# GpSimd waits for its gathers at every second group of tiles in the six edge passes of a graph network kernel

## The chip, the cores and the metric

The kernel runs on one core of one Trainium2 chip. The metric is the device time of a whole execution in microseconds (us). Three runs of the kernel before gave 10969.36, 11014.58 and 11011.19 us; the median is 11011.19 us.

## The reference, cut to what matters

A graph of N = 6250 nodes with 128 float32 features and E = 100000 edges passes through four layers, each fed by a layer norm and a ReLU and added to the running features.

```python
# layer 0: messages by edge type, gated by a sigmoid, summed over the target node, then a GRU cell
msg_in = concat([x[src], x[dst]], axis=1)
h = relu(msg_in @ W1[t] + b1[t]);  m = (h @ W2[t] + b2[t]) * sigmoid(msg_in @ attn_w[t] + attn_b[t])
agg = zeros_like(x).at[dst].add(msgs)
# layer 1: attention over the edges of a row (sorted by src), softmax per row
score = neighs @ high - 0.5 * (neighs @ diff)      # neighs = tanh(x)[dst]; here rows = src
out = segment_sum(neighs * softmax_per_row(score)[:, None], rows)
# layer 2: relations with 8 bases
msg = sum_b w_comp[etype, b] * (x[src] @ weight[b]) * norm;  out = relu(segment_sum(msg, dst) + bias + x @ loop)
# layer 3: three graph convolutions with symmetric degree norm, one after the other
out = segment_sum((x @ W)[src] * norm[:, None], dst) + b
```

Every layer gathers a row of a table for each edge and sums the results per node. Nothing in the change touches what is computed.

## The kernel before, in words

All of it is float32. The kernel first sorts the edges by target window (128 nodes) with counting and scatters them into "slots": 832 tiles of 128 edges, in which each tile belongs to one window; the tiles that are left over at the end are padding, whose slots hold index 0 and a key that matches nothing. A second sort by source serves layer 1. Between the sorts and the passes lie stages that build tables in HBM.

There are six passes over the edges, each a scope of its own with its own semaphores: `edges0`, `edges1`, `edges2`, and `edges3` once for each of three graph convolutions. A pass goes through GROUPS = 208 groups of G = 4 tiles. In each pass GpSimd does nothing but the gathers, through the helper `gather_groups`: for each tile an indirect DMA (line 484) brings 128 rows of a table in HBM into a ring of buffers in SBUF, one row for each of the 128 partitions.

- `edges0` gathers two tables (`rows_s` and `rows_d`, rows of 132 floats, 528 bytes), so eight gathers a group; the ring has R = 4 groups. VectorE adds the two (line 791), ScalarE makes the hidden values (774, 777), VectorE makes one-hot matrices of the target and type (799), TensorE multiplies (851) and VectorE adds the product into the accumulator (815). A slot of the ring is free again when `hidden_done` counts its group.
- `edges1` gathers one table with rows of 528 bytes; the ring has eight groups. ScalarE takes the landed rows first (1133); VectorE, TensorE and ScalarE work out a running softmax. A slot is free with `sums`.
- `edges2` gathers rows of 1024 floats, 4096 bytes (eight bases); the ring has four groups. When a group has landed, ScalarE scales four of the eight parts (1424) and VectorE the others (1447, 1459), VectorE makes the one-hot (1436), TensorE multiplies six parts for each tile (1492), and VectorE adds (1469). A slot is free with `product`.
- `edges3` gathers rows of 128 floats, 512 bytes; the ring has eight groups. TensorE multiplies the one-hot (1602) by the landed rows (1623) and VectorE adds (1612). A slot is free with `product`.

Each slot of the ring has its own semaphore `gathered[slot]`; a gather adds 16 to it when it has landed. The consumers wait until it has reached 16 x (gathers of a group) x (turns of the ring). The order of GpSimd's work is that of its program: for each group the wait for a free slot, then its gathers. The other engines run through the stages of a group as software pipelines with fixed lags, written by `for_groups`.

Of the kernel before, what the change touches and what calls it, by code (L numbers as in the profile page):

```python
# [43 lines left out]
G, R, R1 = 4, 4, 8  # L44
# [387 lines left out]
def wait(engine, semaphore, value):  # L432

    if not isinstance(value, int) or value > 0:
        engine.wait_ge(semaphore, value)
# [39 lines left out]
def gather_groups(pool, ring, freed, gathered, parts):  # L475


    for g in range(GROUPS):
        slot = g % ring
        wait(pool, freed, g - ring + 1)  # L480
        for j in range(G):
            for rows, table, slots, field in parts:
                index = slots[:, G * g + j, field:field + 1].bitcast(I32)
                pool.indirect_dma_start(out=rows[:, slot, j, :], out_offset=None, in_=table[:, :],  # L484
                                        in_offset=bass.IndirectOffsetOnAxis(ap=index, axis=0)).then_inc(gathered[slot], 16)
# [236 lines left out]
def edges0(nc, A, D, K, acc):  # L722


    with Scope(nc, "edge0") as s:
# [31 lines left out]
        @block.gpsimd  # L757
        def _(pool):
            gather_groups(pool, R, q["hidden_done"], gathered,
                          [(rows_s, D["tab_src"], slots, F_SRCT), (rows_d, D["tab_dst"], slots, F_DSTT)])  # L760
# [319 lines left out]
def edges1(nc, D, K, acc):  # L1080
# [5 lines left out]
    with Scope(nc, "edge1") as s:  # L1086
# [28 lines left out]
        @block.gpsimd  # L1115
        def _(pool):
            pool.wait_ge(q["indexed"], 1)
            gather_groups(pool, R1, q["sums"], gathered, [(rows, D["tab1"], slots, 0)])
# [270 lines left out]
def edges2(nc, D, K, acc):  # L1389
# [7 lines left out]
    with Scope(nc, "edge2") as s:  # L1397
# [13 lines left out]
        @block.gpsimd  # L1411
        def _(pool):
            gather_groups(pool, R, q["product"], gathered, [(rows, D["tab2"], slots, F_SRC)])
# [326 lines left out]
```

## Time and profile before

| | |
|---|---|
| median of three runs | 11011.19 us |
| profiled execution | 10982.13 us |
| its span, first to last instruction | 10980.3 us |
| mean granted TensorE clock | 0.708 of full |
| busy: PE, DVE, ACT, POOL | 52%, 48%, 22%, 69% |
| HBM traffic | 80 GB/s over the span |

The engines are named as in the profile: PE is TensorE's matmul and PEld its weight load, DVE VectorE, ACT ScalarE, POOL GpSimd. Busy time leaves out waits. In the span edges0 lies at about 1630 to 3960 us, edges1 at 5045 to 6120, edges2 at 6342 to 7515, and the three layers of edges3 begin at 7607, 8740 and 9880.

### The profile page before, as it was taken

To read this page: it belongs to the slowest core of one execution; us is meant where nothing else is said; L and a number is where in the kernel's file an instruction comes from. 1 tells how busy PE (TensorE), PEld (TensorE's weight loads), DVE (VectorE), ACT (ScalarE), POOL (GpSimd) and SP (SyncE) were. 2 spreads that over 40 slices of the span, in tenths; PEclk is the share of its full clock that TensorE was granted. 3 is DMA by queue.
4 is the path that set the end of the run, shared out by engine and by line. 5 is a ranking of instruction groups with operands and counts; after the bars stand their busy time and mean duration, and the time that the engine had idled before them with its cause. 6 is when DMAs were issued, how large, how long until landed. Compare 5 with 4: busy or idle time off the path is not lost. (4 is left out here: it accounts for less than half of the span.)

```text
span 10980.3 us, 128933 instructions
## 1 busy us (share of the span) xinstructions
PE 5704.4 (52%) x31462; PEld 4939.8 (45%) x31462; DVE 5292.9 (48%) x11473; ACT 2403.8 (22%) x7643; POOL 7613.1 (69%) x7650
## 2 busy tenths in 40 slices
PE   0000646667666667603566689995444344434443
PEld 0000326666666655402555389995333333333332
DVE  6931016555555531134666578886333433343333
ACT  1000101111111111104767378883000000000000
POOL 1276767777777777777777267774777577757775
PEclk9999657888888865556767799997555555555555
DMA  9901122222222210002222399994222322221223
GB/s 21 16 6 24 62 65 50 50 50 50 50 50 50 50 23 2 2 14 49 53 53 53 92 356 382 381 385 145 52 52 52 47 52 52 52 49 52 52 52 53
DMA packets 587441, 879.48 MB, mean 80 GB/s; under 512 B 340739, under 2 KB 377041, under 8 KB 586828
## 3 DMA queue, kind: packets, MB, share of 16 engines
q0 software_dynamic: 329728, 772.96, 24.5%
q1 hardware_dynamic: 257612, 105.52, 10.1%
q14 instruction: 80, 0.66, 0.0%
q8 instruction: 21, 0.34, 0.0%
HBM read 791.80 MB, written 86.16 MB: 80 GB/s over the span
## 5 line engine op out<-in xcount | busy, mean ns | idle before, releaser
L484 POOL DMA_INDIRECT edge_rows<-tab,all_slots x3328 | 3212.8, 965 | 1113.2 <-issue 976.1
L1623 PE MATMUL edge_psum<-edge_rows,edge_onehot 128*128 128x128 f32 x4992 | 1290.8, 440 | 1908.9 <-DMA edge_rows<-tab,all_slots 1694.1
L1623 PEld LDWEIGHTS edge_psum<-edge_rows,edge_onehot 128*128 128x128 f32 x4992 | 1111.1, 328 | 2088.3 <-issue 1874.0
L1612 DVE TENSOR_TENSOR acc_acc<-acc_acc,edge_psum 128x128 f32 x2496 | 716.4, 287 | 2041.4 <-PE edge_psum L1623 1770.9
L851 PE MATMUL edge_psum<-edge_hidden,edge_onehot 128*128 128x130 f32 x6656 | 1176.4, 354 | 800.1 <-ACT edge_hidden L777 794.2
L851 PEld LDWEIGHTS edge_psum<-edge_hidden,edge_onehot 128*128 128x128 f32 x6656 | 1120.9, 264 | 866.1 <-DVE acc_acc L815 754.2
L1492 PE MATMUL edge_p_m<-edge_rows,edge_onehot 128*128 128x128 f32 x9984 | 1130.5, 276 | 46.9 <-ACT edge_rows L1424 42.6
L1492 PEld LDWEIGHTS edge_p_m<-edge_rows,edge_onehot 128*128 128x128 f32 x9984 | 1122.2, 192 | 55.3 <-issue 33.8
L484 POOL DMA_INDIRECT edge_rows_d<-tab_dst,all_slots x832 | 958.0, 1151 | 253.7 <-issue 253.7
L484 POOL DMA_INDIRECT edge_rows_s<-tab_src,all_slots x832 | 852.5, 1025 | 275.3 <-issue 253.4
L1424 ACT ACTIVATE edge_rows<-edge_rows,edge_coef 128x128 f32<-128x128 f32 x3328 | 997.6, 390 | 173.5 <-DMA edge_rows<-tab,all_slots 173.5
L484 POOL DMA_INDIRECT edge_rows<-tab,edge_slots x832 | 811.0, 975 | 262.3 <-issue 253.4
L196 POOL DMA_INDIRECT slots_s<-upd_pay_ring,upd_row_ring x656 | 632.6, 964 | 229.8 <-issue 206.4
L815 DVE TENSOR_TENSOR acc_acc<-acc_acc,edge_psum 128x520 f32 x832 | 576.5, 693 | 310.4 <-PE edge_psum L851 261.4
L1567 ACT ACTIVATE tab_hT<-tab_p_t 128x128 f32<-128x128 f32 x150 | 41.5, 278 | 2273.0 <-PE tab_p_t L1553 2271.3
L1266 PE MATMUL edge_p_u<-edge_rows,edge_prob 128*128 128x129 f32 x1664 | 355.0, 379 | 318.7 <-ACT edge_prob L1159 318.7
L196 POOL DMA_INDIRECT slots_d<-sort_pay_ring,sort_row_ring x320 | 358.3, 1120 | 218.3 <-DMA sort_pay_ring<-pay_d 120.5
L799 DVE TENSOR_TENSOR edge_onehot<-all_iota,all_slots 128x1024 f32<-128x1024 f32 x416 | 507.8, 1221 | 0.0
L1459 DVE SCALAR_TENSOR_TENSOR edge_rows<-edge_rows,edge_coef 128x128 f32<-128x128 f32 x1664 | 487.5, 344 | 0.0
L196 POOL DMA_INDIRECT slots_d<-tab_pay_ring,tab_row_ring x400 | 384.2, 961 | 145.7 <-issue 122.9
L774 ACT ACTIVATE edge_hidden<-edge_rows_s 128x4 f32<-128x4 f32 x208 | 43.9, 211 | 1984.4 <-DVE edge_rows_s L791 1984.4
L1266 PEld LDWEIGHTS edge_p_u<-edge_rows,edge_prob 128*128 128x128 f32 x1664 | 301.2, 271 | 382.9 <-ACT edge_prob L1159 338.5
(250 smaller groups left out, 8590.1 us busy)
## 6 DMA issues: line engine op xcount, KB each, us to landing
edge_rows<-tab,all_slots POOLq DMA_INDIRECT x3328, 2.5
tab<-tab_o SPq DMA_DIRECT2D x50, 512.0 KB, 2.6
edge_rows_s<-tab_src,all_slots POOLq DMA_INDIRECT x832
edge_rows_d<-tab_dst,all_slots POOLq DMA_INDIRECT x832
edge_rows<-tab,edge_slots POOLq DMA_INDIRECT x832, 2.5
tab_src<-tab_oa SPq DMA_DIRECT2D x50, 264.0 KB, 2.1
tab_dst<-tab_ob SPq DMA_DIRECT2D x50, 264.0 KB, 2.2
slots_s<-upd_pay_ring,upd_row_ring POOLq DMA_INDIRECT x656
```

Of the source, the lines that this page charges most:

```text
L196: pool.indirect_dma_start(out=self.table[:, :], out_offset=bass.IndirectOffsetOnAxis(ap=self.row_ring[:, z, j:j + 1], axis=0), in_=self.pa ...
L484: pool.indirect_dma_start(out=rows[:, slot, j, :], out_offset=None, in_=table[:, :], in_offset=bass.IndirectOffsetOnAxis(ap=index, axis=0) ...
L774: act.activation(hidden[:, slot % 2, :, H], rows_s[:, slot, :, H], ACT.Sigmoid).then_inc(q["scored"], 1)
L799: v.tensor_tensor(onehot[:, slot % 2, half * n:(half + 1) * n, :], bcast_mid(K["iota"][:, :], n), bcast_last(slots[:, ds(g * G + half * n, ...
L815: v.tensor_tensor(at, at, psum[:, j % 2, :, 0:2 * SW], ALU.add).then_inc(q["added"], 1)
L851: m = pe.matmul(psum[:, j % 2, t // 2, (t % 2) * SW:(t % 2) * SW + SW], onehot[:, slot % 2, j, t * P:(t + 1) * P], hidden[:, slot % 2, j, ...
L1266: m = pe.matmul(p_u[:, z, j // 2, (j % 2) * HW:(j % 2) * HW + H + 1], prob[:, z, j, :], rows[:, slot, j, 0:H + 1], start=True, stop=True)
L1424: a = act.activation(part, part, ACT.Copy, scale=coef[:, ds(G * g + j, 1), b])
L1459: v.scalar_tensor_tensor(first, rows[:, slot, j, b * H:(b + 1) * H], coef[:, ds(G * g + j, 1), b], first, ALU.mult, ALU.add).then_inc(q["c ...
L1492: m = pe.matmul(at, onehot[:, z, j, :], rows[:, slot, j, b * H:(b + 1) * H], start=(n == 0), stop=(n == len(PARTS) - 1))
L1612: v.tensor_tensor(at, at, psum[:, slot % 2, j * P:(j + 1) * P], ALU.add).then_inc(q["added"], 1)
L1623: m = pe.matmul(psum[:, slot % 2, j * P:(j + 1) * P], onehot[:, slot % 2, j, :], rows[:, slot, j, :], start=True, stop=True)
```

## The change

In `gather_groups`, ahead of the gathers of each even group but the first, GpSimd waits until all gathers of the group before have landed, by the semaphore of that group's slot. All six passes use the helper.

```diff
 def gather_groups(pool, ring, freed, gathered, parts):
+    each = 16 * G * len(parts)
     for g in range(GROUPS):
         slot = g % ring
         wait(pool, freed, g - ring + 1)
+        if g and g % 2 == 0:
+            pool.wait_ge(gathered[(g - 1) % ring], each * ((g - 1) // ring + 1))
         for j in range(G):
             for rows, table, slots, field in parts:
```

`len(parts)` is 2 in edges0 and 1 elsewhere.

## Rows read from the trace of the kernel before

**Rows 1.** The page's costliest groups: line, engine, count, busy us, mean ns, idle before.

```profile
L484 POOL DMA_INDIRECT edge_rows<-tab,all_slots x3328 | 3212.8, 965 | 1113.2 <-issue 976.1
...
L484 POOL DMA_INDIRECT edge_rows_d<-tab_dst,all_slots x832 | 958.0, 1151 | 253.7 <-issue 253.7
L484 POOL DMA_INDIRECT edge_rows_s<-tab_src,all_slots x832 | 852.5, 1025 | 275.3 <-issue 253.4
```

**Rows 2.** GpSimd's waits in edges0 and edges2: us in total, times, longest.

```profile
POOL edge_rows_d L484 <- issue: 253.7, 832, 0.3
...
POOL edge_rows L484 <- PE edge_p_m L1492: 97.6, 123, 8.8
```

**Rows 3.** Timeline in edges3: start us, us, instruction, idle before it.

```profile
8601.30 0.95 POOL L484 DMA_INDIRECT edge_rows<-tab,all_slots  x1 [0.30 <-issue]
8602.56 0.96 POOL L484 DMA_INDIRECT edge_rows<-tab,all_slots  x1 [0.30 <-issue]
...
8604.06 2.07 PE L1623 MATMUL edge_psum<-edge_rows,edge_onehot 128*128 128x128 f32 x8 [2.95 <-DMA edge_rows<-tab,all_slots]
```

**Rows 4.** Busy by stage: edges0, edges2, second layer of edges3.

```profile
core 0: us, PE busy (x) PEld busy (x) DVE busy (x) ACT busy (x) POOL busy (x), PEclk, DMA share, GB/s
1630.00:3960.00 2330.00, 1591.26 (x9973) 1495.92 (x9974) 1355.47 (x1871) 331.69 (x1248) 1810.47 (x1664) 0.80 0.23 50
6342.00:7500.00 1158.00, 1118.62 (x9884) 1110.78 (x9885) 979.14 (x2885) 991.39 (x3308) 834.56 (x832) 0.99 0.99 379
8740.00:9790.00 1050.00, 426.13 (x1648) 366.78 (x1648) 370.28 (x1029) 0.00 (x0) 791.02 (x832) 0.50 0.22 52
```

**Rows 5.** The same view, 200 us in the middle of edges2.

```profile
6642.00:6842.00 200.00, 197.00 (x1741) 195.07 (x1740) 171.18 (x507) 174.16 (x581) 148.06 (x146) 1.00 0.99 381
```

**Rows 6.** Gathers' landing: 6400 to 7400; the one at 6372.17; third layer of edges3.

```profile
DMA to landing us min/median/max: 5.1/5.9/7.3
...
DMA to landing us min/median/max: 5.1/5.1/5.1
...
DMA to landing us min/median/max: 2.4/2.5/12.7
```

**Rows 7.** Timelines of one group's last gather in edges0, then in edges1.

```profile
2610.16 0.95 POOL L484 DMA_INDIRECT edge_rows_d<-tab_dst,all_slots  x1 [0.31 <-issue]
...
2612.61 0.71 DVE L791 TENSOR_TENSOR edge_rows_s<-edge_rows_s,edge_rows_d 128x528 f32<-128x528 f32 x1 [2.44 <-DMA edge_rows_d<-tab_dst,all_slots]
2612.66 1.47 POOL L484 DMA_INDIRECT edge_rows_d<-tab_dst,all_slots  x1 [0.30 <-issue]
...
5060.27 0.94 POOL L484 DMA_INDIRECT edge_rows<-tab,edge_slots  x1 [0.30 <-issue]
...
5062.77 1.28 ACT L1133 ACTIVATE edge_score<-edge_other,edge_rows 128x128 f32<-128x128 f32 x4 [1.58 <-issue]
```

**Rows 8.** Timeline in edges2 after GpSimd's longest wait.

```profile
6372.00 1.23 DVE L1447 TENSOR_TENSOR edge_rows<-edge_rows,edge_coef 128x1024 f32<-128x1024 f32 x1 [4.42 <-PE edge_p_m L1492]
6372.17 1.88 POOL L484 DMA_INDIRECT edge_rows<-tab,all_slots  x1 [8.77 <-PE edge_p_m L1492]
...
6382.28 0.94 POOL L484 DMA_INDIRECT edge_rows<-tab,all_slots  x1 [0.30 <-issue]
...
6389.22 0.99 ACT L1424 ACTIVATE edge_rows<-edge_rows,edge_coef 128x128 f32<-128x128 f32 x3 [0.27 <-DMA edge_rows<-tab,all_slots]
```

**Rows 9.** Busy in single microseconds around that wait, columns as in rows 4.

```profile
6366.00:6367.00 1.00, 1.00 (x7) 1.00 (x6) 1.00 (x6) 1.00 (x5) 0.00 (x0) 0.50 1.04 422
6371.00:6372.00 1.00, 1.00 (x12) 1.00 (x11) 0.00 (x0) 1.00 (x5) 0.00 (x0) 1.00 1.07 430
6373.00:6374.00 1.00, 1.00 (x12) 1.00 (x11) 1.00 (x4) 0.72 (x3) 1.00 (x1) 1.00 0.05 20
6378.00:6379.00 1.00, 1.00 (x12) 1.00 (x11) 1.00 (x3) 0.63 (x3) 0.83 (x1) 1.00 0.90 315
```

## The prediction

> **What bounds the kernel now.** I read the costliest groups first, then the busy times by stage, then what GpSimd waited for in each stage, and last the timelines around one group. The chain that ended last is of no use here: it holds only VectorE's last operations. The gathers are the largest items of the page: 3328 of edges2 and the three layers of edges3, and 2 x 832 in edges0 [rows 1]. The reader is to see in their idle column that nearly all of it is "issue", 0.30 us between two gathers with nothing awaited; in edges0 that holds for all 832 gathers of one of its two tables [rows 2]. So a gather costs about 0.95 + 0.30 = 1.25 us of GpSimd [rows 3], and in edges0, edges1 and edges3 GpSimd sets the pace: a layer of edges3 has 832 gathers in 1050 us, PE 41% and DVE 35% busy, DMA 22% [rows 4]. PE, DVE and ACT wait there for landings.
>
> Edges2 is another regime. Its rows are 4 KB (eight times those of edges3), the DMA engines are 99% busy at 379 GB/s and PE is 97% busy [rows 4]; 146 gathers in 200 us are 1.37 us each [rows 5], so two groups (8 gathers) take 10.96 us. A gather lands 5.9 us after its start in the median [rows 6], so some four are in flight. GpSimd's own slack is small: it waits for PE 123 times, 97.6 us in all [rows 2].
>
> **The change, part by part.** 832 tiles in groups of four are 208 groups. The wait stands at g = 2, 4, ... 206: 103 waits a pass, 618 in the six passes (edges0, edges1, edges2, edges3 three times). It asks that group g-1, issued directly before, has landed whole. Queued behind it are the gathers of g and g+1 and nothing else; their landings release DVE (edges0), ACT (edges1), ACT and DVE (edges2), PE (edges3). Nothing is removed. The wait instruction itself I put at nothing.
>
> *Edges0, edges1, edges3.* A wait costs the time from the start of a group's last gather to the restart, less the 1.25 us after which the next gather starts anyway. In edges0 the last gather starts at 2610.16 and DVE, which waits for it, at 2612.61: 2.45 us [rows 7]. In edges1 ACT starts 2.50 us after it [rows 7]. In edges3 PE starts 2.76 us after it [rows 3]. GpSimd's own waking the trace shows only after PE: released together with DVE it starts 0.17 us later [rows 8]. So the restart comes 2.62 to 2.9 us after the last start and the wait costs 1.37 to 1.7 us; the landing cannot be had before 2.4 us [rows 6], which makes 1.2 us the lower end. I take 1.40 in edges0 and edges1 (the DVE and ACT rows) and 1.45 in edges3 (between them and PE's, nearer to the former): 206 x 1.40 + 309 x 1.45 = 288 + 448 = 736 us; the ends are 515 x 1.2 = 618 and 515 x 1.7 = 876.
>
> Could the pause pay something back? In edges0 gathers take 1151 and 1025 ns in the mean instead of 947, because some start while VectorE works: the one at 2612.66, 0.05 us after DVE L791, takes 1.47 us [rows 7]. All of that is 832 x (0.204 + 0.078) = 235 us, the most that could come back. But the restart comes with the very landing that starts L791, so it meets that operation as before. I count nothing, up or down. At the end of a pass the padding tiles land late, up to 12.7 us [rows 6], DMA-bound in both kernels; there a drain costs about as much, over three or four waits.
>
> *Edges2.* Here the wait empties the DMA queue once in two groups. The trace has one such stop: GpSimd waited 8.77 us and started again at 6372.17 [rows 8]; in the microsecond from 6373 the DMA engines were 5% busy with 20 GB/s, and six microseconds after the restart they gave 315, not 381 [rows 9, 5]. The first gather took 1.88 us beside DVE L1447 and landed 5.1 us after its start [rows 6, 8]. The eighth started at 6382.28, and ACT, which waited for it, at 6389.22, 17.05 us after the restart [rows 8]. That is the upper end for two groups with waking: 17.2. The lower: first landing at 5.1, less 0.93 if DVE doesn't lengthen it, seven more at 1.37, and 0.15 for waking: 13.9. With the lengthened restart it is 14.85. I take 16.05, nearer to the only measured stop, where further gathers were already queued behind the eighth. So 16.05 - 10.96 = 5.1 us, x 103 = 525 us; the ends are 303 and 643.
> PE then idles several us in a pair, as in edges0, where its granted clock averages 0.80 [rows 4]. At half clock it began 7 matmul records in a microsecond against 12 at full [rows 9]: the 96 of two groups would take about 14 us, still under 16. The ring of four groups covers the delay. If a pair took 13.9, that cover would be gone.
>
> **Two rules of the notes against the rows.** Beside a DVE tensor_tensor two gathers took 1.88 and 1.47 us [rows 7, 8], against 0.95 alone [rows 3]. The Trainium skill, "SBUF — State Buffer", section "Who interferes with whom", infers that a tensor_tensor does not hold up descriptor generation. By that the restart in edges2 would be 0.93 us shorter, 96 us less in all; the trace disagrees.
> The Trainium skill, "DMA: Bandwidth & Descriptors", section "Anatomy of one DMA — SWDGE (gpsimd) path", gives about 2.0 us plus the bytes at 436 GB/s for one DMA. For 64 KB that is an estimate of 2.15 us; the rows show 2.4 to 2.5. By the page the 515 short waits would cost about 1.07 us each, 551 us instead of 736.
>
> **Sum.** 736 + 525 = 1261 us on the profiled execution's 10982.1 us: 12243. That execution lies 0.3% under the median of the runs, 11011.2, which I leave aside. What is late next is again GpSimd, through landings; nobody else comes near.
>
> **Rivals.**
> 1. *The DMA queue hardly notices the drain in edges2.* For it: 1.37 us a gather is bandwidth and the eight gathers are queued within some 10 us. Against: 315 GB/s after the stop. A pair of 13.9 to 14.85, say 14.4, gives 354 instead of 525: 12070.
> 2. *Restarting is dearer.* The 0.30 us of issue may be paid anew after each wait, and edges2 may take its 17.2. For: PE's 2.76. Against: the restart at 6372.17 follows DVE by 0.17. 12243 + 515 x 0.25 + 118 = 12490.
> 3. *No slower.* The gathers of the group behind hold up the landing of the one before, since the same engine makes their descriptors; left alone, a gather would land by the time at which the next would start. The place is every wait; it decides where the landing comes within 1.25 + 0.09 us of the start (55 us over 618 waits). Then edges2 too would have to lose nothing. Against: DMA is 22% busy in edges3, landings don't vary with what is queued, 2.4 at least. The time would be 10980, or less by some of the 235 us of collisions.
> 4. *The wait does nothing*, the semaphore's count being reached earlier than meant. But the consumers wait for the same counts, and they do wait. 10982.
>
> **Chances and range.** Forecast 0.68 (own range 12100 to 12400), rival 1 0.14, rival 2 0.13, rivals 3 and 4 0.05 together. The bounds summed are 10982 + 618 + 303 = 11903 and 10982 + 876 + 643 = 12501; the range 11900 to 12510 takes in rivals 1 and 2. Within 0.5% (55 us, about what a measurement of this kernel can tell) 0.03, faster 0.02, slower 0.95.
>
> **What would show it.** In the profile after, idle time of GpSimd ahead of gathers, released by DMA, 103 times a pass, some 1.7 us each with the 0.30 (1.1 us for edges3 at the least would be below my bound); an edges3 layer of about 1190 us instead of 1040; edges2 of about 1680 us with the DMA share near 0.7 and PE's clock below 1; gathers still 947 ns in edges3. I am wrong where a layer of edges3 grows by under 120 or over 175 us, or edges2 by under 300 or over 650.

## The result and the profile after

The changed kernel takes 12613.3 us in the median (12597.5 to 12633.4, four runs) against 10992.9 us (10969.4 to 11014.6, four runs) of the kernel before: a ratio of 1.148, with a 95% interval of 1.144 to 1.151. The forecast was 12243 us with a range up to 12510. The sign was right; the growth is 1620 us where 1261 were forecast.

The page's costliest groups of the changed kernel, columns as in rows 1. The `wait` and the gathers stand at L488 now, four lines further down.

```profile
L488 POOL DMA_INDIRECT edge_rows<-tab,all_slots x3328 | 3237.5, 973 | 2362.5 <-DMA edge_rows<-tab,all_slots 1385.6
...
L488 POOL DMA_INDIRECT edge_rows_s<-tab_src,all_slots x832 | 852.6, 1025 | 488.5 <-DMA edge_rows_d<-tab_dst,all_slots 240.9
...
L488 POOL DMA_INDIRECT edge_rows_d<-tab_dst,all_slots x832 | 884.4, 1063 | 280.5 <-issue 280.5
```

GpSimd works hardly longer than before (3237.5 us for 3212.8 in the first group); its idle time ahead of the gathers has grown from 1113 to 2363 us in the first group, and "issue" has given way to "DMA" as what ends it [rows 1]. In edges0 the gathers of the second table have become shorter, 1063 ns for 1151 [rows 1].

Busy by stage of the changed kernel, for the stretches of rows 4: edges0, edges2, second layer of edges3.

```profile
1645.00:4127.00 2482.00, 1586.48 (x9901) 1490.22 (x9902) 1345.60 (x1859) 329.61 (x1243) 1734.97 (x1663) 0.78 0.21 47
6723.00:8448.00 1725.00, 1317.37 (x9875) 1298.05 (x9876) 970.11 (x2876) 985.35 (x3296) 838.84 (x832) 0.86 0.72 254
9921.00:11198.00 1277.00, 426.68 (x1649) 367.28 (x1650) 371.71 (x1033) 0.00 (x0) 797.61 (x832) 0.50 0.18 43
```

All three are longer with the same work in them. Edges2 went from 99% to 72% of the DMA engines and from 379 to 254 GB/s, and PE's granted clock there from 0.99 to 0.86 [rows 4]. From the start of a pass's first gather to that of its last, in us:

```
            before   after   growth  forecast
edges0      2316.1  2481.9    165.8      144
edges1      1063.4  1272.4    209.0      144
edges2      1148.6  1725.1    576.5      525
edges3 (1)  1044.0  1277.2    233.2      149
edges3 (2)  1043.5  1276.6    233.1      149
edges3 (3)  1048.1  1279.5    231.4      149
```

The growths sum to 1649 us; the two profiled executions differ by 12610.1 - 10982.1 = 1628. So the passes hold all of it, and 21 us came back outside them. They grew by 388 us more than the 1261 forecast, 336 of these in the five passes with short waits and 52 in edges2.

### The profile page after: what moved, and what is told of

The parts are those of the page before. It is cut to its first block and busy times, and to the rows that moved or that the text cites. A ratio compares the mean times of both kernels' runs of the same rounds, so it can differ in the third digit from the quotient of the medians.

```text
span 12608.3 us, 129537 instructions
## 1 busy us (share of the span) xinstructions
PE 5993.7 (48%) x31462; PEld 5180.9 (41%) x31462; DVE 5279.4 (42%) x11473; ACT 2390.8 (19%) x7643; POOL 7551.3 (60%) x7650
## 5 line engine op out<-in xcount | busy, mean ns | idle before, releaser
L488 POOL DMA_INDIRECT edge_rows<-tab,all_slots x3328 | 3237.5, 973 | 2362.5 <-DMA edge_rows<-tab,all_slots 1385.6
L1496 PE MATMUL edge_p_m<-edge_rows,edge_onehot 128*128 128x128 f32 x9984 | 1331.6, 303 | 417.7 <-ACT edge_rows L1428 229.5
L1496 PEld LDWEIGHTS edge_p_m<-edge_rows,edge_onehot 128*128 128x128 f32 x9984 | 1312.0, 218 | 437.3 <-DVE acc_acc L1473 397.6
L488 POOL DMA_INDIRECT edge_rows_s<-tab_src,all_slots x832 | 852.6, 1025 | 488.5 <-DMA edge_rows_d<-tab_dst,all_slots 240.9
L488 POOL DMA_INDIRECT edge_rows<-tab,edge_slots x832 | 794.1, 954 | 488.0 <-issue 233.9
L488 POOL DMA_INDIRECT edge_rows_d<-tab_dst,all_slots x832 | 884.4, 1063 | 280.5 <-issue 280.5
L1451 DVE TENSOR_TENSOR edge_rows<-edge_rows,edge_coef 128x1024 f32<-128x1024 f32 x208 | 254.9, 1225 | 762.7 <-DMA edge_rows<-tab,all_slots 730.0
L1270 PE MATMUL edge_p_u<-edge_rows,edge_prob 128*128 128x129 f32 x1664 | 384.2, 402 | 288.9 <-ACT edge_prob L1163 288.9
L1234 DVE SCALAR_TENSOR_TENSOR acc_acc<-acc_acc,edge_ratio,edge_scaled 128x129 f32 x832 | 289.1, 347 | 547.1 <-ACT edge_scaled L1155 542.8
L795 DVE TENSOR_TENSOR edge_rows_s<-edge_rows_s,edge_rows_d 128x528 f32<-128x528 f32 x208 | 148.6, 714 | 824.5 <-DMA edge_rows_d<-tab_dst,all_slots 824.5
```

The lines of the kernel that those rows point to most:

```text
L1234: v.scalar_tensor_tensor(this, last, ratio[:, slot % 4, 0, j:j + 1], scaled[:, slot % 2, j, :], ALU.mult, ALU.add).then_inc(q["added"], 1)
L1270: m = pe.matmul(p_u[:, z, j // 2, (j % 2) * HW:(j % 2) * HW + H + 1], prob[:, z, j, :], rows[:, slot, j, 0:H + 1], start=True, stop=True)
L1496: m = pe.matmul(at, onehot[:, z, j, :], rows[:, slot, j, b * H:(b + 1) * H], start=(n == 0), stop=(n == len(PARTS) - 1))
```

## What one wait looks like

Timeline of the changed kernel in edges3, around a wait.

```profile
8687.59 0.95 POOL L488 DMA_INDIRECT edge_rows<-tab,all_slots  x1 [0.30 <-issue]
8688.84 0.94 POOL L488 DMA_INDIRECT edge_rows<-tab,all_slots  x1 [0.30 <-issue]
...
8691.60 2.07 PE L1627 MATMUL edge_psum<-edge_rows,edge_onehot 128*128 128x128 f32 x8 [2.94 <-DMA edge_rows<-tab,all_slots]
8692.10 0.94 POOL L488 DMA_INDIRECT edge_rows<-tab,all_slots  x1 [2.32 <-DMA edge_rows<-tab,all_slots]
8693.35 0.94 POOL L488 DMA_INDIRECT edge_rows<-tab,all_slots  x1 [0.31 <-issue]
```

The last gather starts at 8688.84, and PE, which waits for the same landing, 2.76 us later, just as in rows 3. GpSimd starts 0.50 us after PE. The prediction had it restart before PE, 2.70 us after the last gather's start; it is 3.26.

Between the landing and the gather the trace has an instruction that the kernel before has nowhere in its passes. One line's instructions in the changed kernel (L484 is the added `wait_ge`): count, then ns min/median/max, first and last start in us.

```profile
L484 POOLq EVENT_SEMAPHORE  x604: 17/17/17, 1691.7 to 12545.5; - x151
```

There are 604, for 618 waits. The record of such an instruction starts 0.02 us after the last landing, so GpSimd is awake at once; PE starts 0.23 us after the landing, and the gather 0.74 us (medians of the three edges3 layers). A gather that opens a group here has a wait of its own, for a free slot of the ring. Where it also gets the added one, the two become a semaphore instruction and a gather behind it: the instruction carries the wait that the code issues last, for the landing (its line is L484), and the gather keeps the one issued first, for the slot. At the start of a pass no slot has to be free yet: there the added wait is alone on the gather, in one restart each of edges0 and edges2 and in three of each other pass (1 + 1 + 4 x 3 = 14). Timeline of such a restart, in the changed kernel at the start of edges3:

```profile
8568.48 0.94 POOL L488 DMA_INDIRECT edge_rows<-tab,all_slots  x1 [0.30 <-issue]
8571.34 0.94 POOL L488 DMA_INDIRECT edge_rows<-tab,all_slots  x1 [1.93 <-DMA edge_rows<-tab,all_slots]
```

The first three restarts of an edges3 layer have 1.77 to 1.93 us of idle time and start 0.26 us after the landing, the others have 2.31 in the median and start 0.74 after it. That difference, some 0.47 us, became the theory that the last experiments test.

## The experiments

They ran in three groups (e1 to e4, e5 to e8, e9 to e12), each on one chip. There the kernel before itself took 12924, 13065 and 12880 us, not 10993. So ratios hold within a group; what is slower there stands with e9 below. Where no ratio with an interval is given, the times are those of a single execution. All kernels come from one generalised `gather_groups`, with a setting per pass: at every which group it waits, for the group how far back, ahead of which gather of the group (`j == at`), and on what.

```
for g in range(GROUPS):
    wait(pool, freed, g - ring + 1)
    for j in range(G):
        if every and g and g % every == 0 and g >= lag and j == at:
            pool.wait_ge(gathered[(g - lag) % ring], each * ((g - lag) // ring + 1))
        ...
```

**e1_wake.** What GpSimd waits on, in edges3; every fourth group in edges2.

```
-  pool.wait_ge(gathered[...], ...)
+  layer 1: pool.wait_ge(relay, g)       # ScalarE waits for the gathers and counts up
+  layer 2: pool.wait_ge(freed, g)       # PE's product of the group
+  layer 3: pool.wait_ge(gathered[...], ...); pool.memset(probe[:, g // 2:g // 2 + 1], 0.0)
```

> Edges0 and edges1 as in the changed kernel. In the changed kernel GpSimd restarts 0.5 to 0.6 us after the engine that waits for the same landing. Theory A (dispatch): after any blocking wait the gather behind it pays its issue time again, whoever released it. Theory B (source): GpSimd sees a DMA's count late, but not another engine's. Layer 1 of edges3: ScalarE waits for each landing and passes it on, GpSimd waits for ScalarE. A: restart 3.1 us or more after the last gather's start, first to last gather 1280 us or more (changed kernel 1277). B: restart at about 2.75, some 1225 us. Layer 2: the wait is for TensorE's product of the group before. A: GpSimd restarts 0.5 us after VectorE, which waits for the same product; B: 0.1 us. Either way the layer grows to some 1430 to 1470 us. Layer 3: the wait is followed by a memset of one column on GpSimd and then the gather. A: memset 0.1 to 0.2 us after TensorE could start, the gather 0.3 us behind its end; B: memset at 3.1 us after the last gather's start, gather at 3.5. Edges2: wait at every fourth group, batches of 16 gathers. If a drain costs a fixed time and then DMA runs at 1.37 us a gather, a batch takes 16.75 + 8 x 1.37 = 27.7 us and the pass 1440 us; if the rate stays near the 250 GB/s of the changed kernel, 33 us and 1720.

Timeline of e1_wake in layer 3: the memset behind the wait shows when GpSimd is awake.

```profile
12511.26 0.10 POOL L492 MEMSET edge_probe<- 128x1 f32 x1 [1.73 <-DMA edge_rows<-tab,all_slots]
12511.37 1.78 PEld L1645 LDWEIGHTS edge_psum<-edge_rows,edge_onehot 128*128 128x128 f32 x8 [3.42 <-issue]
12511.38 2.07 PE L1645 MATMUL edge_psum<-edge_rows,edge_onehot 128*128 128x128 f32 x8 [3.13 <-DMA edge_rows<-tab,all_slots]
12511.92 0.95 POOL L495 DMA_INDIRECT edge_rows<-tab,all_slots  x1 [0.56 <-issue]
```

GpSimd is awake 0.12 us before PE starts, and the gather comes 0.56 us after the memset's end. From the last gather's end to the restart it is 2.35 us in the median with the memset in it, and 2.33 without, in edges1: the memset fits into it. So the engine is not woken late; the gather needs the time after the wake. The relay through ScalarE did not help (2.37 us; the pass 1284 us, layer 3's 1285). Waiting for PE's product took 4.64 us, 2.31 more than a wait for the landing, and PE's matmuls alone are 2.07 of these. GpSimd restarts 0.60 us after VectorE, which waits for the same product (median), where theory A had 0.5 and B 0.1. So the delay does not depend on who releases the wait. The pass took 1520 us, above the 1430 to 1470 expected: that expectation had left too little for the matmuls. Edges2 with half of the waits took 1538 us.

**e2_lag2.** All passes wait for the group before the last.

```
-  gathered[(g - 1) % ring], each * ((g - 1) // ring + 1)
+  gathered[(g - 2) % ring], each * ((g - 2) // ring + 1)
```

> All six passes: at every second group GpSimd waits for the landing of the group two before, not one before. The last gather of that group started five gathers (6.2 us) earlier and lands in 2.5 us in five passes, so the count is there when the wait is reached. If only the blocked time costs: 10990, ratio 1.000, edges2 unchanged too, since up to twelve gathers may be in flight where four to five are. Rival: the wait instruction costs by itself, up to the 0.3 us of an issue: 618 x 0.3 = 185 us, ratio up to 1.017.

12891.7 us against 12923.5, a ratio of 0.998 (0.995 to 1.001). The trace has the 604 semaphore instructions here too. The ratio alone could hide a small cost, as GpSimd is not always the pace on this chip. But in edges3's layer 1 the gather behind an added wait has the plain 0.30 us of idle time in 74 of 103 cases, and the group's first gather without one in 77 of 104. So a wait that is met when GpSimd comes to it costs nothing measurable, its extra instruction included.

**e3_late.** Edges0, edges1, edges2 and edges3's layer 3 wait at every group, layer 1 after one gather of the new group, layer 2 after two.

```
edges0, edges1, edges2, edges3 (3):  every = 1
edges3 (1):  every = 2, at = 1
edges3 (2):  every = 2, at = 2
```

> Edges0, edges1 and edges2: a wait at every group (207 a pass). Edges3 layer 1: at every second group, but after one gather of the group is out; layer 2: after two gathers; layer 3: at every group. If the cost is the 3.15 us from the last gather's start to the restart, less the gathers issued meanwhile at 1.25 us: layer 1 103 x 0.65 = 67 us and the padding tiles, 1115 to 1130 from first to last gather; layer 2 nothing but the padding tiles, 1044 to 1060; layer 3 207 x 1.93 = 400, some 1450 to 1480; edges1 1063 + 415 = 1480; edges0 2316 + 207 x 2.0 less the collisions with VectorE that fall away (73 us at 103 waits) = 2580 to 2650. Edges2 in batches of four: with a fixed cost of a drain and 1.37 us a gather 16.75 - 5.5 = 11.3 us a batch, 2350 us; if a batch's rate is what sags, 9.5 to 10 us, 2000 to 2080.

14168 us. Layer 3 took 1499 us, 14.43 us for two groups against 10.05 before, so 2.19 us a wait. Layers 1 and 2 took 1190 and 1185 us, not the 1115 to 1130 and 1044 to 1060 expected; on this chip e2_lag2, whose waits cost nothing, has 1180. Edges0 and edges1 took 2605 and 1491 us, as expected. Edges2 took 2273 us, 10.9 us for a drained group of four.

**e4_without_edges2.** The change in the other five passes.

> The change in all passes but edges2. By the traces edges2 grew by 577 us of the 1626: 12040 here. If the passes influence each other (a clock, a later stage) it would be off by more than 30 us.

13051 us, not 12040: the kernel before takes 12924 here. Edges2 kept its 1326 us (1325.8 in e2_lag2 too): the five passes' waits charge it nothing.

**e5_without_edges2 and e6_only_edges2.** The same kernel timed, and its complement, on the second chip.

> The wait of the change in all passes but edges2 (its GpSimd program is that of the kernel before). Theory A, the 577 us by which edges2 grew are its own and the other five passes bring 2.0 to 2.2 us per wait: 1.6% to 1.7% for each of edges3's three passes and 1.5% for edges1 and 0.7% to 1.5% for edges0, together 1050 us, the whole kernel at 1.09 to 1.10 times the kernel before, and edges2 at its old length. Theory B, edges2 is charged partly by its neighbours' stalls: the ratio stays below 1.08 and edges2 still grows. Where the kernel before is itself held up on this chip by other engines than GpSimd, both shrink.

> The wait in edges2 alone. Theory A: 577 us over the kernel before, 1.050 to 1.055 of it, and the two ratios' excesses (this and the one without edges2) add to that of the whole change, 0.148. Theory B: the two don't add, by over 0.01 (each part hides some of the other's).

Ratios of 1.006 (1.004 to 1.008) and 1.029 (1.024 to 1.034). Both are far below what theory A says (1.09 to 1.10 and 1.050 to 1.055), and they cannot decide between A and B. Edges3's layers took 1275 to 1279 us with the waits, as in the first measurement, but 1190 without them, not 1044: on this chip most of what a wait costs is lost already without it. The first of the two expectations had left that open.

**e7_probe.** Memsets without a wait (layer 1), two behind the wait (layer 2), half of the waits (layer 3 and edges2).

```
 layer 1:
-  pool.wait_ge(gathered[...], ...)
+  pool.memset(probe[:, g // 2:g // 2 + 1], 0.0)
 layer 2:
   pool.wait_ge(gathered[...], ...)
+  pool.memset(probe[:, g // 2:g // 2 + 1], 0.0)
+  pool.memset(probe[:, 104 + g // 2:105 + g // 2], 0.0)
```

> Four small changes, a pass each: edges0 as before; edges2 waits at every fourth group; in edges3's layer 1 no wait at all, but a 128x1 GpSimd memset in the same place at every second group; in layer 2 the wait followed by two such memsets; in layer 3 the wait at every fourth group. Theory A (GpSimd wakes as soon as the other engines, and the first gather then needs about 0.56 us of its own, because nothing ran ahead of it to hide that): the first memset after the wait starts 1.7 us after the last gather's end, the second right behind it, the gather 0.56 after the second, so layer 2's wait is dearer by one memset (0.1 us) than with one. In layer 1, with the memset between gathers, two answers tell where the 0.56 is from: if any instruction of another kind ahead of a gather costs it, each memset costs 0.10 plus 0.56 in place of 0.30, some 0.4 us, 40 us in the pass; if only an engine that was idle pays it, 0.1 us each, 10 us. Theory B (GpSimd is woken late by 0.6 us): the two memsets start late together. Layer 3: half of the waits, half of the 222 us. edges2: 1537.9 us was seen on the slower chip; on a chip where GpSimd is the pace 27.7 us per sixteen gathers, 1440 us, if only the drain is paid twice as seldom.

Timeline of e7_probe in layer 1, where GpSimd didn't stop.

```profile
9813.59 0.94 POOL L499 DMA_INDIRECT edge_rows<-tab,all_slots  x1 [0.30 <-issue]
9814.52 0.12 POOL L488 MEMSET edge_probe<- 128x1 f32 x1
9814.84 1.16 POOL L499 DMA_INDIRECT edge_rows<-tab,all_slots  x1 [0.19 <-issue]
```

And in layer 2, behind the wait.

```profile
11014.71 0.10 POOL L494 MEMSET edge_probe<- 128x1 f32 x1 [1.61 <-DMA edge_rows<-tab,all_slots]
11014.74 0.10 POOL L496 MEMSET edge_probe<- 128x1 f32 x1
...
11014.83 2.07 PE L1640 MATMUL edge_psum<-edge_rows,edge_onehot 128*128 128x128 f32 x8 [2.95 <-DMA edge_rows<-tab,all_slots]
11015.39 0.94 POOL L499 DMA_INDIRECT edge_rows<-tab,all_slots  x1 [0.55 <-issue]
```

Without a stop the memset lies inside the 0.30 us between two gathers and costs nothing (0.18 us of idle time behind it in the mean), less than either answer expected (0.4 or 0.1 us). The simplest reading is that what a gather needs ahead of its start goes on while the instruction before it runs. After a stop it is not hidden: 0.55 us behind the last memset. That is theory A, and B (woken late) is out, since both memsets start ahead of PE. Layer 3 and edges2 with half the waits took 1204 and 1554 us; the first shows nothing, as layer 1, without waits, has 1191 here.

**e8_place.** The places of e3_late again, edges0 and edges1 without waits.

```
edges2, edges3 (3):  every = 1
edges3 (1):  every = 2, at = 1
edges3 (2):  every = 2, at = 2
```

> Where the wait stands. edges0 and edges1 without it. edges2 at every group: if each drain costs a fixed 5.4 us over the 5.5 us of its four gathers, 10.9 us per group, 2270 us. edges3: layer 1 waits after one gather of the new group, layer 2 after two, layer 3 at every group. Theory A: after one gather 1.25 us of the 3.55 are covered and the idle is 2.3 less 1.25, so 1.0 us and some 75 to 85 us of growth over 1044 in the pass; after two nothing is left, 1044 to 1050 us; at every group twice the 222 us, 1490. Theory B (each blocking wait is dear whatever is left of the landing): after one gather 150 us or more.

Timeline of e8_place in layer 1: the wait stands between two gathers of a group.

```profile
10706.55 0.94 POOL L499 DMA_INDIRECT edge_rows<-tab,all_slots  x1 [0.30 <-issue]
10708.06 0.94 POOL L499 DMA_INDIRECT edge_rows<-tab,all_slots  x1 [0.56 <-DMA edge_rows<-tab,all_slots]
```

Where the landing ends it, the idle time after one gather is 0.54 us in the median (0.59 in e3_late), not the 1.0 expected from 2.3 - 1.25. It is near 1.84 - 1.25 = 0.59. In the middle of a group the added wait has the gather for itself, since the one for the slot stands at the group's first. This miss, with the three short restarts above, gave the theory its form. After two gathers nothing is left at the wait (0.30 us in the median). The two layers' times, 1201 and 1195 us, say nothing, as a layer without waits has 1191 on this chip (e7_probe). Every group: 1490 us as expected, and edges2 2277.

**e9_before_again.** The kernel before out of the same source, for a trace on the chip of the next three.

```
HOW: every = 0 in all passes
```

> The kernel before, from the changed source with the wait left out, to have a trace of it from the chip on which the experiments run. Nothing is expected of it but the time of the kernel before on this chip; where that is again above 12800 us, the passes of edges3 should show GpSimd held up for 1.0 us or so at the group's first gather by groups that PE has not freed, and a pair of groups taking 11.4 us in place of 10.05.

12882 us. What VectorE waited for in edges3's layer 1, us in total, times and longest; e9_before_again:

```profile
DVE acc_acc L1630 <- remote: 645.6, 84, 20.2
DVE acc_acc L1630 <- PE edge_psum L1641: 46.6, 47, 2.8
```

The same view of the kernel before, first measurement:

```profile
DVE acc_acc L1612 <- PE edge_psum L1623: 578.5, 205, 4.6
```

"Remote" is a release that the trace attributes to no engine. VectorE is held by such ones for up to 20 us, and GpSimd runs into the end of its ring; two groups take 11.37 us in the mean, as expected. Both wait there for `product`, PE's count. VectorE's first addition of a group starts 5.28 us in the median after the record of the group's last matmul has ended, once 33.9 us; in the kernel before, first measurement, it is 0.15 us in all 208 groups, and with the change on the chip of e9 (e10_change_again) 0.15 again. So PE's count comes late, and why the traces do not show. A layer of edges3 takes 1180 us in place of 1044, and the whole kernel 17% more; some 700 of those 1900 us lie outside the passes.

**e10_change_again and e11_early.** The change, and the change with the slot's wait one gather earlier.

```
-    wait(pool, freed, g - ring + 1)        # ahead of a restarting group
     for j in range(G):
+        if j == G - 1 and (g + 1) % 2 == 0:
+            wait(pool, freed, g + 1 - ring + 1)
```

> The change itself, on the chip of the experiments. If edges3, edges1 and edges2 are bound there by the same chain of waits as in the first measurement, their passes take the same 1276, 1275 and 1720 us whatever the kernel before does; where the kernel before is slower on this chip because its other engines stall, the ratio must be smaller than 1.148: about 1.03 to 1.04, the 1.006 without edges2 and the 1.029 with edges2 alone together.

> The change with one wait moved in all passes: where GpSimd waits for all gathers, the other wait, for a free slot of the ring, stands one gather earlier, so that the restarting gather carries a single wait. The trace of the changed kernel has a 17 ns semaphore instruction of GpSimd's in front of the restarting gather (604 of them, none in the kernel before), absent only at the first three waits of a pass, where no slot has to be free yet; those three restart 1.81 to 1.93 us after the last gather's end, the others 2.25 to 2.35. Theory A (0.45 us of each restart is the split into a semaphore instruction and a gather that starts only then): every restart is 1.8 to 1.9 us, the semaphore instructions are gone, and a pass of edges3 takes 46 us less than with the change, 1230 us. Theory B (the first three are quick because the pass has just begun): nothing changes, 2.3 us and 1276.

Ratios of 1.039 (1.035 to 1.043) and 1.028 (1.023 to 1.032): one wait moved by one gather takes 143 us off, 13398.6 to 13255.6. The change's ratio and its passes (1283, 1281 and 1719 us for layer 1, edges1 and edges2) came as expected. In e11_early the semaphore instructions are gone. What GpSimd waited for in edges3's layer 1, first e10_change_again, then e11_early.

```profile
POOL edge_rows L501 <- DMA edge_rows<-tab,all_slots: 248.1, 102, 7.0
POOL edge_rows L501 <- issue: 236.9, 729, 2.6
```

```profile
POOL edge_rows L501 <- issue: 203.2, 665, 0.4
POOL edge_rows L501 <- DMA edge_rows<-tab,all_slots: 200.6, 103, 6.3
```

A restart has 1.86 us of idle time in place of 2.34, all through the pass and not only at its start, and the gather behind it 0.30 in place of 0.42 in the mean: 0.60 us a restart. (The 0.42 is 0.30 in 91 of 100 cases and 1.67 in nine, at every eleventh restart; why is open.) The layer is 39 us shorter, not 60, because its fourth gather now meets VectorE more often (1.28 us in the mean, 1.05 with the change). The timeline of e11_early shows GpSimd level with PE:

```profile
10012.75 0.95 POOL L501 DMA_INDIRECT edge_rows<-tab,all_slots  x1 [1.87 <-DMA edge_rows<-tab,all_slots]
10012.75 1.57 PEld L1641 LDWEIGHTS edge_psum<-edge_rows,edge_onehot 128*128 128x128 f32 x7 [3.37 <-issue]
10012.75 1.64 PE L1641 MATMUL edge_psum<-edge_rows,edge_onehot 128*128 128x128 f32 x6 [3.08 <-DMA edge_rows<-tab,all_slots]
```

Edges2 gained nothing (1719 and 1726 us). Its restarting gather is earlier and so lies beside a VectorE tensor_tensor, 1.93 us in the mean where it was 1.30 in e10_change_again. The slot's wait, one gather earlier, is not always met there: the last gather before a stop has 1.04 us of idle time in place of 0.30, and the restart 5.11 in place of 6.31.

**e12_order.** The slot's wait earlier (edges0, layer 2), or behind the other (edges1, layer 1); edges2 waits after two gathers.

```
 layer 1, edges1:
-  wait(pool, freed, g - ring + 1)
   pool.wait_ge(gathered[...], ...)
+  wait(pool, freed, g - ring + 1)
```

> Five passes tell the order and the place apart. edges0 and edges3's layer 2: as in the run before, the slot's wait one gather earlier; edges3's layer 1 and edges1: both waits in front of the restarting gather, the one for the slot second; edges3's layer 3: the change. Theory A: only the pair of waits matters, in whatever order: layer 1 and edges1 with 2.3 us, unless the late one is now carried by the gather itself and the met one by the semaphore instruction: then 1.85 us. Layer 2 at 1.85, layer 3 at 2.3. edges2: the wait stands after two gathers of the new group, for the groups before. If what makes edges2's wait dear is only the landing of its last gathers, two gathers cover 2.9 us of 6.2, 3.3 us are left, 1400 to 1450 us of pass; if it is the queue of 64 KB gathers that runs empty and has to fill again, it is nearer to 1600.

Busy by stage of e12_order: edges2 (after two gathers), layer 1 (swapped), layer 3 (the change).

```profile
7523.00:8921.00 1398.00, 1203.23 (x9861) 1168.36 (x9862) 974.71 (x2877) 985.93 (x3298) 890.88 (x832) 0.96 0.90 313
9031.00:10274.00 1243.00, 426.14 (x1648) 366.78 (x1648) 370.04 (x1033) 0.00 (x0) 820.32 (x831) 0.50 0.19 44
11682.00:12966.00 1284.00, 426.54 (x1649) 367.21 (x1650) 369.48 (x1033) 0.00 (x0) 802.00 (x832) 0.50 0.19 42
```

Restarts have 1.84 us of idle time in layer 1, 1.85 in layer 2 and 2.31 in layer 3 (medians), and edges1, swapped too, took 1241 us for 1281. Swapping two lines is enough: the semaphore instruction then carries the slot's wait, now issued last and met in advance, and the gather the late one. It is the second of the two answers that the expectation allowed. The instruction itself is still there in 91 of layer 1's 103 restarts, so it is dear only where it is the one that blocks. Edges2 with two gathers in flight over the wait took 1398 us, just under the 1400 to 1450 expected of the landing alone, against 1719 with the change and 1325 without a wait (e9_before_again). As the queue never runs empty here, this does not tell the landing's share of edges2's price from that of refilling the queue.

## Why the prediction fell short

**What bounds the kernel** held. GpSimd's wait sets the pace in every pass, PE, DVE and ACT wait for landings, and GpSimd's idle time ended by a DMA is there 102 or 103 times a pass (90 in edges1, where the trace names PE for the rest).

**The step that failed** is "GpSimd's own waking", 0.17 us after DVE [rows 8], together with "The wait instruction itself I put at nothing". By them a short wait was to cost 1.40 or 1.45 us; the 515 of them cost 1073 us, 2.08 each. The landing was read rightly: PE starts 2.76 us after the last gather [rows 3], and so it does after. But 0.17 us came from a restart with one wait on the gather, released along with DVE. The code shows that the restarting gather already carries `wait(pool, freed, ...)`. With a second wait one of the two becomes an instruction of its own, and where that is the one that blocks, the gather starts 0.74 us after the landing, not 0.26. Measured per restart: 0.47 us more idle time, and 0.12 on the next gather. That the gather is prepared during its own wait, but only behind a semaphore instruction that blocks, is the reading that fits all runs; the preparation itself no trace shows.

In an edges3 layer, over the 149 us forecast: the split 100 x 0.59 = 59 us; the landing with a single wait, 1.85 us of idle time against the 1.75 that the forecast implies, 10 us; the padding tiles at the end of the pass, where three waits took 3.5, 6.2 and 6.3 us, 9 us; together 78 of the 84 us missing. In the five passes the split makes an estimated 502 x 0.59 = 296 us, against 336 missing, from which edges0's payback of 73 (below) is already taken. The first two of these terms are measured in e10 to e12; that they have the same size in the first measurement follows from its own trace (2.31 us and 1.77 to 1.93), where no kernel without the split ran.

**Rival 2, restarting dearer,** was the true case. It named the mechanism nearly as it is, issue paid anew, and gave it 0.25 us and a chance of 0.13. With 0.59 in place of 0.25 its sum is 12665, against 12610 measured in that execution; its 118 us for edges2 were 52, and it had no payback in edges0. The evidence held against it, the restart at 6372.17, was a restart of another kind.

**Edges0** grew by 166 us and nearly met its 144 by luck, as two errors cancel. Idle time brought 103 x 2.05 = 211 us and 103 x 0.26 = 27 on the next gather. The collisions paid back 832 x 0.088 = 73. The forecast counted no payback, since "the restart comes with the very landing that starts L791". It comes later. Timeline of the changed kernel in edges0, DVE's operation after the landing (L791 is L795 now) and GpSimd's restart:

```profile
2600.52 0.71 DVE L795 TENSOR_TENSOR edge_rows_s<-edge_rows_s,edge_rows_d 128x528 f32<-128x528 f32 x1 [3.63 <-DMA edge_rows_d<-tab_dst,all_slots]
...
2601.26 0.94 POOL L488 DMA_INDIRECT edge_rows_s<-tab_src,all_slots  x1 [2.30 <-DMA edge_rows_d<-tab_dst,all_slots]
```

But L791 is not where the collisions are. The row with 1.47 us [rows 7] is a rare one: in the kernel before, 64 gathers of edges0 start under L791 and 21 of them take over 1.2 us, while 426 start under L799, VectorE's one-hot, and 273 of them do. Timeline of the kernel before, a group's fourth gather:

```profile
2203.04 1.22 DVE L799 TENSOR_TENSOR edge_onehot<-all_iota,all_slots 128x1024 f32<-128x1024 f32 x1
...
2203.36 1.72 POOL L484 DMA_INDIRECT edge_rows_d<-tab_dst,all_slots  x1 [0.30 <-issue]
```

The stop shifts a restarting group against that operation: over 1.2 us took 6 of its fourth gathers where it was 86 of 104, none of its seventh where it was 39, but 44 of its fifth where it was 2. The restarting gather itself has 0.94 us in the mean, 0.95 before.

**Edges2** took 16.59 us for two groups, forecast 16.05, within its ends of 13.9 and 17.2. Timeline of the changed kernel there, around a restart:

```profile
7407.88 1.23 DVE L1451 TENSOR_TENSOR edge_rows<-edge_rows,edge_coef 128x1024 f32<-128x1024 f32 x1 [1.12 <-DMA edge_rows<-tab,all_slots]
7408.48 1.43 POOL L488 DMA_INDIRECT edge_rows<-tab,all_slots  x1 [6.41 <-DMA edge_rows<-tab,all_slots]
```

DVE and GpSimd are released by the same landing, and GpSimd starts 0.60 us later, not 0.17. The gather takes 1.43 us, not 1.88, for it overlaps DVE less. So e11_early, which cures the delay, brings the collision back and nothing is won. Rival 1 (the queue hardly notices) was wrong here: its 14.4 us for two groups were 16.59, with 6.36 us of idle time a wait.

**Rivals 3 and 4** had no part in it. That gathers are "still 947 ns in edges3" held nearly (959), and the named condition of being wrong, a layer growing by over 175 us, came true with 233.

## What to carry to other kernels

Before pricing an added wait, look at which waits its instruction already has. Two on one gather became two instructions: the wait that the code issues last went into the semaphore instruction in front, the one issued first stayed on the gather. So issue the wait that comes late first and the one that is met already last (e12_order), or move the latter to an earlier instruction, if it is met there too (e11_early). A wait that is met costs nothing. One that is not costs the time to the landing of the last transfer, less that of the gathers issued behind it. Leaving two gathers in flight took most of the price away: 73 us of edges2's 394 were left. No version with waits was faster than the kernel without.

## What the runs showed of the hardware

- A 128x1 GpSimd memset between two gathers is free: it lies inside the 0.30 us between them (e7_probe). Behind a stop, with a semaphore instruction in front, the next gather starts 0.55 us after the memset's end.
- A stop by a wait on the gather itself gives 1.84 us of idle time, by a semaphore instruction in front of the gather 2.31 (e10_change_again). Two ways of keeping the blocking wait on the gather give the same 1.84 (e11_early, e12_order).
- In edges2, whose rows are 4 KB [rows 4], four gathers issued and landed by themselves take 10.9 us, eight 16.6 us, sixteen 29.7 to 30.0 us (e8_place, the changed kernel, e1_wake and e7_probe): 1.4 us for each further gather from four to eight, and 1.6 to 1.7 from eight to sixteen, where the two chips' own pace without waits is 1.6 (12.8 us for eight in e2_lag2). Four at 1.4 leave some 5 us that every drain costs anew.
- The changed kernel's edges1, edges2 and edges3 took nearly the same time in the first measurement and in e10_change_again (1277 and 1283 us for layer 1, 1725 and 1719 for edges2), while the kernel before took 17% more beside the latter, and the changed one 6%. The same edit cost 14.8% in the one and 3.9% in the other, for a reason that lies mostly in the kernel before: PE's count of finished groups, for which VectorE and GpSimd wait, comes late there. What delays it, and whether it goes with the chip or with the moment, stays open.
